# ScalarE copies the transposed probabilities of the first three sequences of the window-attention phase

## The reference, cut to what matters

```python
h = shift_token(x)
q, k, v = split(h @ wqkv)                 # to 8 heads of 64
q, k = rotary(l2norm(q) * qs, l2norm(k) * ks)
sim = q @ k.T * 8                          # own window of 128 and the one before it
attn = softmax(where(mask, -max, sim))
x = x + (attn @ v) @ wo
h = layernorm(shift_token(x)) * lg + lb
a, g = split(h @ w1 + b1)
x = x + (a * gelu(g)) @ w2 + b2
```

## Time and profile before

| what | us |
|---|---|
| median of 3 runs | 1282.58 (1274.68 to 1283.24) |
| the profiled execution | 1282.97 |
| its span | 1281.1 |
| TensorE busy | 1211.2 (95%) |
| VectorE busy | 989.2 (77%) |
| ScalarE busy | 860.8 (67%) |
| GpSimd busy | 621.7 (49%) |

### The profile page before, as it was taken

How to read it: one execution, slowest core, us unless ns; L and a number is a source line. 1 busy time by engine, 2 the same in 40 slices (tenths; PEclk the granted TensorE clock), 3 DMA queues, 4 the chain that set the end, 5 groups by cost and what they waited for, 6 DMA issues and landing times.

```text
span 1281.1 us, 26137 instructions
## 1 busy us (share of the span) xinstructions
PE 1211.2 (95%) x8899; PEld 1030.5 (80%) x8899; DVE 989.2 (77%) x2624; ACT 860.8 (67%) x1989; POOL 621.7 (49%) x678
## 2 busy tenths in 40 slices
PE   5899999999999999799988889999999999999998
PEld 4699989888888889567766567888788888888898
DVE  5766666666667776789888888888888888888754
ACT  2455765676566556679974568777777777777764
POOL 6423351352145233446434567557654667556543
PEclk9899999999999999989988899999999999999999
DMA  7400020001000000310010002000100000000001
GB/s 172 113 1 15 2 65 0 14 33 33 0 8 1 1 1 1 76 48 18 18 53 17 1 6 94 5 6 4 47 5 6 22 5 13 22 14 21 22 10 42
DMA packets 39615, 33.25 MB, mean 26 GB/s; under 512 B 16774, under 2 KB 36178, under 8 KB 39506
## 3 DMA queue, kind: packets, MB, share of 16 engines
q1 hardware_dynamic: 38610, 29.74, 7.7%
q0 software_dynamic: 768, 2.10, 1.0%
q10 hardware_dynamic: 128, 0.04, 0.0%
HBM read 25.84 MB, written 4.19 MB: 23 GB/s over the span
## 4 chain that ended last, share of the span: by engine, by line
PE 47%; DVE 5%; issue 3%; POOL 2%; ACT 2%; DVEq 0%; ACTq 0%; POOLq 0%
PE w_ps_p L1911 3%; PE w_ring L1870 3%; PE w_ring L1972 3%; PE w_ring L1872 3%; PE w_ring L1871 3%; PE w_ring L1973 3%; PE w_ring L1974 3%; PE w_ps_a L1929 2%; PE w_ring L1984 2%; PE a_ps L924 2%; PE w_ring L1888 2%; PE w_ps_d L1904 2%; PE w_ps_d L1901 2%; PE w_ring L1985 2%; PE w_ring L1988 1%
## 5 line engine op out<-in xcount | busy, mean ns | idle before, releaser
L392 ACT ACTIVATE t_gf<-t_ps_f,t_fb_cur 128x512 f32<-128x512 f32 x128 | 87.9, 687 | 165.8 <-PE t_ps_f L298 161.4
L311 PE MATMUL t_ps_o<-t_w_hi,t_g_hi 128*128 128x256 f32 x512 | 145.1, 283 | 3.2 <-DVE t_g_lo L542 3.1
L542 DVE TENSOR_TENSOR t_g_lo<-t_gf,t_g_hi 128x512 fp32r<-128x512 f32 x128 | 94.3, 738 | 68.1 <-ACT t_g_hi L394 67.8
L312 PE MATMUL t_ps_o<-t_w_lo,t_g_hi 128*128 128x256 f32 x512 | 143.4, 280 | 0.0
L313 PE MATMUL t_ps_o<-t_w_hi,t_g_lo 128*128 128x256 f32 x512 | 143.3, 280 | 0.0
L695 POOL TENSOR_TENSOR t_rs<-t_ve,t_neghalf 128x4 f32<-128x4 f32 x32 | 40.2, 1258 | 163.2 <-DVE t_ve L503 161.7
L296 PE MATMUL t_ps_f<-t_nh,t_w_hi 128*128 128x512 f32 x256 | 102.7, 401 | 1.4 <-DVE t_nl L518 0.8
L2985 POOL TENSOR_TENSOR w_m<-w_m 128x512 f32<-128x512 f32 x64 | 84.2, 1315 | 40.9 <-DVE w_m L2628 40.7
L311 PEld LDWEIGHTS t_ps_o<-t_w_hi,t_g_hi 128*128 128x128 f32 x512 | 96.6, 189 | 7.6 <-issue 4.4
L298 PE MATMUL t_ps_f<-t_nl,t_w_hi 128*128 128x512 f32 x256 | 100.6, 393 | 0.0
L297 PE MATMUL t_ps_f<-t_nh,t_w_lo 128*128 128x512 f32 x256 | 100.3, 392 | 0.0
(11 more groups left out here) (369 smaller groups left out, 4292.1 us busy)
## 6 DMA issues: line engine op xcount, KB each, us to landing
t_raw<-in_L_tok_w SPq DMA_DIRECT2D x8, 1024.0 KB, 5.2
out<-X SPq DMA_DIRECT2D x14, 256.0 KB, 2.1
raw<-in_L_ffn_wqkv SPq DMA_DIRECT2D x2, 1536.0 KB, 6.8
raw<-in_L_ffn_w SPq DMA_DIRECT2D x4, 640.0 KB, 5.1
w_raw_o<-out SPq DMA_DIRECT2D x8, 256.0 KB, 2.9
w_xs<-X SPq DMA_DIRECT2D x14, 127.0 KB
w_raw<-in_L_ffn_w SPq DMA_DIRECT2D x2, 640.0 KB
t_raw_d<-in_L_tok_D SPq DMA_DIRECT2D x4, 256.0 KB
```

What stands on the lines that cost most here:

```text
L311: pe.matmul(out, g_hi[:, j % 4, tok], w2_hi[:, j, :], start=(j == 0 and t % 2 == 0), stop=False, skip_group_check=True)
L312: pe.matmul(out, g_hi[:, j % 4, tok], w2_lo[:, j, :], start=False, stop=False, skip_group_check=True)
L392: act.activation(gf[:, j % 2, :], ps_f[:, j % 2, :], ACT.Gelu, bias=fb_cur[:, j:j + 1]).then_inc(pf_free, 1)
L542: dve.tensor_tensor(g_lo[:, j % 4, :], gf[:, j % 2, :], g_hi[:, j % 4, :].bitcast(F32), ALU.subtract).then_inc(g_split, 1)
```

## The change

The copy `turned_p(k)` of items 0 to 23 (`BY_SCALAR = 3 * H`, that is the sequences 0, 1 and 2) is made by ScalarE instead of VectorE. Its waits and its signal are the same. ScalarE's copies stand at eight places of its `half(h)`. Items from 24 on stay with VectorE. TensorE's and GpSimd's programs are not changed.

```diff
+    BY_SCALAR = 3 * H
...
+            def turned_p(k):                        # scalar
+                if not 0 <= k < BY_SCALAR:
+                    return
+                if k >= PTS:
+                    act.wait_ge(S["pv_done"], (k - PTS) // 2 + 1)
+                act.wait_ge(S["p_full"], k + 1)
+                act.activation(pt[:, k % PTS, :], ps_p[:, 0, 0:SC], ACT.Copy).then_inc(S["pt_done"], 1)
...
                     hi_1(0, 1)
+                turned_p(H * d + 3)
                 if real(b):
                     squares(b, 0, 0, 0)
+                turned_p(H * d + 4)
                 if real(g):
                     hidden_hi(g, 2)
                 if real(d):
                     probabilities(H * d + 6)
+                turned_p(H * d + 5)
                 if real(b):
                     squares(b, 0, 1, 1)
                 if real(d):
...
                     turned(b, 0, 0, 0)
+                turned_p(H * d + 6)
                 if real(g):
                     hidden_hi(g, 5)
...
                     squares(b, 1, 1, 3)
...
                     affine(f, 2)
+                turned_p(H * d + 7)
                 if h == 5:
                     hi_1(0, 0)
...
                     hi_o(0)
+                turned_p(H * c + 0)
                 if real(c):
                     probabilities(H * c + 4)
+                turned_p(H * c + 1)
                 if h == M + 1:
                     return
...
                     hidden_hi(f, 0)
+                turned_p(H * c + 2)
                 if real(b) and h != 1:
                     keep_values(b, 1, 2)
...
             def turned_p(k):                        # vector
+                if k < BY_SCALAR:
+                    return
                 if k >= PTS:
                     dve.wait_ge(S["pv_done"], (k - PTS) // 2 + 1)
```

## The result

| kernel | median us | runs |
|---|---|---|
| before | 1281.86 | 6, 1274.68 to 1283.57 |
| changed | 1312.38 | 5, 1309.82 to 1314.63; a sixth took 2992.3, for a reason that isn't known, and is left out of every comparison |

The ratio is 1.025, with a 95% interval of 1.0235 to 1.0265. The profiled execution took 1311.78 us with a span of 1310.0, 28.8 us more than that of before.

A forecast was written before the change was run, and what follows sets the result against it. No engine alone bounds the changed stretch; TensorE leaves 12.5 us in waits there and bounds what follows. Terms -1.1 + 7.8 + 9.65 + 2.1 + 5.5 - 2.3 + 2.6 = +24.25 gave 1307.2 us, range 1289 to 1317.

The forecast's parts named there:

- the clock: TensorE in the changed stretch: one net drop from 2.4 to 1.2 GHz after new lulls, +2.6 us.
- what TensorE gets back: Old TensorE waits, such as 1.06 us at 744.55, find their work done: -2.3 us.
- copies 5, 6 and 23: Halves 3 to 5: ready ScalarE work queues behind waiting copies, delaying TensorE: +7.8, +9.65 and +5.5 us.
- copies 8 and 16: Halves 3 and 4: copies stand behind ScalarE's logarithm, in half 3 also the weights' upper part: 1.7 and 0.4, +2.1 us.
- half 2: Copies 0 to 2 leave VectorE ahead of its input split, so TensorE enters half 3 sooner: -1.1 us.
- ScalarE waits in order: ScalarE can't pass a waiting copy, so work behind it is held; if it could, only the gain would be left.
- The copy's own price: One ScalarE copy of 384 columns, start to start: 0.45 us, ends 0.35 and 0.58.
- Copy 3: Finds its transposition done and costs nothing, covered by TensorE's projection after it.
- three lulls: New TensorE idle times of 3.5 to 4.7 us, behind copies 6 of halves 3 and 4 and copy 23.
- Every lull lowers the clock: Rival: three clock drops in the stretch in place of one, +5.2 us, so 1312.4 us; 23 in 100.
- The delays share their slack: Rival: a late ScalarE shortens the next wait, about half of 25.05 us left, +9.1, 1292 us; 18 in 100.
- VectorE is the bound: Rival: not slower; VectorE reaches its splits 1.1 us sooner, four times, -4.4, 1278.6 us; 4 in 100.

The follow-up runs named there:

- the waits alone: Against the kernel before: VectorE makes all copies, ScalarE keeps only 15 waits for transpositions at the places of copies 3 to 7, computing nothing; 1317.36 us, ratio 1.0298.
- kernel with late places: Against the changed kernel: all 24 copies stay on ScalarE, but copies 4 to 7 and 0 stand later, behind work ready earlier; 1278.74 us, ratio 0.9988 to before.
- run with TensorE kept busy: Against the changed kernel: TensorE does 12 useless matmuls ahead of its wait for the third scores in halves 3 and 4; 1308.71 us, ratio 1.022 to before.

## Why the prediction was right, and what was mis-sized

It named the sign, the mechanism and the places; 1307.2 was forecast, 1312.4 measured, inside the range of 1289 to 1317. In the traces the stretch cost 29.7 us where the sum has 24.25. The 5.5 us between them are +2.8 for the clock, +2.3 for what TensorE gets back, +1.4 for copies 5, 6 and 23, -0.6 for the own part of copies 8 and 16 and -0.4 for half 2.

*ScalarE waits in order, and the places decide.* Right, and shown twice: the waits alone cost 37 us, and the same copies in other places cost nothing. No part of the load was seen in either.

*The copy's own price* of 0.45 us start to start: the row is 0.49 long, the next instruction starts 0.38 to 0.39 later (809.08 to 809.47). Right enough.

*Copies 5, 6 and 23.* 22.95 us were forecast and 24.3 measured, each step within 0.35 us and most of them higher. The chains written out from the rows of before were the chains that ran, with one reservation. The 0.9 forecast for GpSimd behind copy 23 came as 0.72, but its scaling ended at 815.26 and TensorE, at the lower clock, reached `turn_p(24)` at 815.31 without a wait, so either could have set that time.

*Copy 7 in halves 3 and 4* had no term. By itself it costs 3.4 and 3.2 us, by the run with it alone; it hardly counted because copy 6's chain covers it but for 0.3 us. The sum was right there without the argument for it having been made, which is luck.

*Copy 3* was put at nothing, since it "finds its transposition done". In half 5 that failed. Item 19's transposition was done at 777.95, but ScalarE was at the weights' upper parts, which stand ahead of the copy in its order. In the kernel before, VectorE copied this item 1.5 us after its transposition had begun (766.93 to 768.41); now it is 4.1 us. TensorE, then ScalarE, in the changed kernel:

```profile
777.40 0.55 PE L1912 MATMUL w_ps_p<-w_ident,w_pr 128*128 128x128 f32 x3
...
782.12 0.52 PE L1912 MATMUL w_ps_p<-w_ident,w_pr 128*128 128x128 f32 x3 [0.96 <-ACT w_pt L2363]
```

```profile
780.16 1.44 ACT L2299 ACTIVATE w_w_hi<-raw 128x1492 fp32r<-128x1492 f32 x1
781.50 0.48 ACT L2363 ACTIVATE w_pt<-w_ps_p 128x384 f32<-128x384 f32 x1
```

The lag grows by 1.1 us there. Here the copy is what comes late, and not the work behind it. The kernel with late places leaves copy 3 where it is and has the same wait, 0.97 us.

*Copies 8 and 16* were forecast at 2.1 and measured at 4.1. The run with TensorE kept busy gives 2.6 of it to the clock (0.7 and 1.9): without the lower clock the two steps would be 1.2 and 0.3.

*What TensorE gets back* was forecast at -2.3 and came to nothing. Old waits did go, 1.9 us of them, most between `turn_p(9)` and `turn_p(12)`. But two new ones had no term: the 1.1 us of copy 3 in half 5, and 0.8 in half 3, where the second `scores` waited for VectorE's `soft` of the late first ones (0.75 us at 724.04).

*The clock is the mis-sized term.* "I take one net" put 2.6 us on it, after listing three lulls. In the changed kernel the clock stood at the lower level six times in this stretch, where in the kernel before it did so once. The stretches, columns as in rows 2:

```profile
728.00:735.00 7.00, 4.74 (x25) 3.05 (x27) 5.42 (x25) 4.75 (x20) 3.04 (x4) 0.51 0.00 1
752.00:755.50 3.50, 3.50 (x14) 2.62 (x11) 3.40 (x12) 0.60 (x1) 2.91 (x4) 0.51 0.02 5
765.50:772.50 7.00, 6.16 (x31) 3.82 (x31) 4.30 (x21) 3.54 (x15) 4.26 (x5) 0.51 0.07 18
789.50:793.00 3.50, 3.50 (x16) 2.50 (x13) 3.40 (x11) 2.13 (x5) 3.29 (x4) 0.51 0.00 0
803.00:807.00 4.00, 4.00 (x23) 4.00 (x22) 1.36 (x7) 0.00 (x0) 0.00 (x0) 0.57 0.04 11
813.50:820.50 7.00, 6.79 (x34) 4.43 (x35) 5.54 (x22) 6.89 (x17) 6.86 (x7) 0.51 0.64 229
```

The first, third and last go with the lulls of the list. The others follow lulls that weren't on it: 3.44 us ahead of `scores` by copy 5 in halves 4 and 5, and 3.75 ahead of the feed-forward's first matmul. By the granted clock TensorE stood at the lower level for 6 us between 700 and 800 before (0.03 of 100, twice) and for 20 us there and 10 us more to 820 after. Lower clock is paid only where TensorE has work: 24 us more of it can cost 12 us at most. Measured are 5.4 us in steps where TensorE ran on without a wait (1.55 to `turn_p(14)`, 0.33 to `turn_p(18)`, 1.59 to `turn_p(23)`, 1.90 to `turn_p(26)`) and the 2.6 in copies 8 and 16, less the 2.6 that the old drop gave back: 5.4 net, double the term. The fourth stretch cost nothing, since TensorE had idled 1.25 us there before.

The Trainium skill ("TensorE: Matmul & The Clock Gate", HAM oscillation), cited in the prediction for three drops, says that the cost is paid again for each idle gap. The trace agrees in six of its seven lulls of 3.44 us and more; the first, at 719.60, was followed by full clock.

*Every lull lowers the clock*, the rival with 23 in 100, forecast 1312.4 us, and that this is the measured median is partly luck. Its three drops came, and three more. But it counts 7.8 us for the clock where 5.4 net were paid, and keeps the 2.3 us given back that didn't come; the two errors cancel.

*The rivals.* "The delays share their slack" is refuted for the terms of the sum: 24.3 us of the copies' steps were paid in full. "VectorE is the bound" is refuted by VectorE's busy time, 60 of 100 us where it was 86, with no gain. That nothing lost here would be made up behind it was right: the lag doesn't change by more than 0.01 us through the next full half.

*Half 2's gain* of 1.1 came as 1.5. It is the part of the change that is worth having: the kernel with copies 0 to 2 alone keeps it, 2 us by the medians. The 2.6 us of the absent drop at 712 us were luck of the profiled execution, and the kernels that miss it or have it don't differ in half 2: from `turn_p(0)` to the first projection of half 3 it takes 7.03 to 7.04 us in the five traces with copies 0 to 2 on ScalarE, and 8.54 to 8.55 in the five others.

**Behind and before the stretch.** The lag grows once more, from 27.22 to 28.74 us, behind an idle time of 1.79 us that both traces have (at 1116.04 and, in before, at 1088.81). It is the clock again, first the changed kernel, then before:

```profile
1117.00:1121.00 4.00, 4.00 (x15) 3.27 (x15) 3.44 (x15) 1.35 (x4) 2.78 (x5) 0.57 0.01 4
```

```profile
1090.00:1094.00 4.00, 4.00 (x23) 3.19 (x22) 4.00 (x15) 2.39 (x9) 3.26 (x5) 1.00 0.02 4
```

In the phases before the change, too, the lag moves where the clocks differ. From 545 to 570 us, with 0.83 granted in before and 1.00 in the changed kernel from 540 on, it falls from 1.0 to -2.3 us.

**Left open.** How much of the 2.5 us by which these phases differ is the clock's wasn't separated; the runs of before alone spread by nine. Why the clock falls after one lull and not after another of the same length wasn't tried.

## What to carry to other kernels

Work that is moved to an emptier engine joins that engine's order, and its wait comes along: for each new place, look up in the trace when the awaited thing ends and when the instructions behind it ran, and write the chain from the first of them to the next instruction that TensorE awaits. A busy share says nothing on this; here TensorE's, VectorE's, ScalarE's and GpSimd's all fell in the stretch, and the kernel got slower. Look both ways in each half: copy 3 cost nothing in two halves and 1.1 us in the third, where other work stood ahead of it. And a place that fits where the pipeline fills need not fit where it is full, for the same reason.

## What the runs showed of the hardware

One fall of TensorE's clock to its lower level cost about 2.5 us when it lasted over 6 us and dense work followed: 2.58 by the rows of before (5.88 against 3.30), 2.5 and 2.6 in the kernel with copy 5 alone. Shorter ones cost 1.5 to 1.6 (in the changed kernel behind `scores` at 751.39, behind the feed-forward's matmul at 802.71, and at 1117). Where TensorE waited anyway it cost less: 0.7 us behind 730.26, nothing behind 789.17.

They came behind idle times of 3.44, 3.57, 3.75, 4.38 and 4.73 us, and once of 1.79. But the 3.44 us in half 3 of the changed kernel were followed by matmuls at full clock (0.49 us at 719.60) and the 3.44 us of the kernel with copy 5 alone by 0.80: the same lull, the other outcome. The lull ahead of 712 us had three outcomes in ten traces. From the first projection of half 3 to `turn_p(4)` it took 5.9 us in two of them, 4.9 in four, and 3.3, at full clock, in four.
